# Attention and butterfly FFN on one core: the sums split into 64-key parts, one per row half of TensorE's array

## The reference, cut to what matters

```python
qkv = (x @ W_qkv + b_qkv).reshape(B, D, 3, H, p).transpose(2, 0, 3, 1, 4)
q, k, v = (qkv[0], qkv[1], qkv[2])
scores = jax.nn.softmax(jnp.einsum('bhip,bhjp->bhij', q, k), axis=-1)
out = jnp.einsum('bhij,bhjp->bhip', scores, v)
...
x = x + _L0_attn_ref(xn, ...) + _L0_ffn_ref(xn, ...)
```

## Time and profile before

| | us |
|---|---|
| median of 3 runs | 5605.22 |
| span of the profiled execution | 5607.5 |
| TensorE matmul busy | 5554.5 (99%) |
| ScalarE busy | 5021.6 (90%) |
| VectorE busy | 4884.1 (87%) |
| POOL busy | 527.8 (9%) |
| scores L1041, union busy, 8192 matmuls | 2058.5 |
| pieces L1019 without the difference, 7049 | 2497.4 |
| sums L1055, 16384 instructions | 2184.2 |
| exps L774, 8192 | 4222.8 |
| reductions L847, 6042 | 3958.3 |

### The profile page before, as it was taken

How to read it: one execution, slowest core, us unless ns; L and a number is a source line. 1 busy time by engine, 2 the same in 40 slices (tenths; PEclk the granted TensorE clock), 3 DMA queues, 4 the chain that set the end, 5 groups by cost and what they waited for, 6 DMA issues and landing times.

```text
span 5607.5 us, 98374 instructions
## 1 busy us (share of the span) xinstructions
PE 5554.5 (99%) x36132; PEld 2628.7 (47%) x36132; DVE 4884.1 (87%) x9092; ACT 5021.6 (90%) x9744; POOL 527.8 (9%) x482
## 2 busy tenths in 40 slices
PE   7899999999999999999999999999999999999999
PEld 6644444444444444444444444444444444444698
DVE  7799999999999999999999999999999999998233
ACT  6699999999999999999999999999999999999644
POOL 2436652000000000000000000000000000000000
PEclk9899999999999999999999999999999999999999
DMA  8702221111110111111111011111111101110111
GB/s 297 218 25 48 58 58 29 17 19 21 21 21 8 21 21 21 21 15 21 21 21 20 8 21 21 21 21 15 21 21 21 17 10 21 21 21 2 35 45 41
DMA packets 212351, 197.12 MB, mean 35 GB/s; under 512 B 149288, under 2 KB 170152, under 8 KB 200104
## 3 DMA queue, kind: packets, MB, share of 16 engines
q1 hardware_dynamic: 208432, 168.05, 15.9%
q0 software_dynamic: 3456, 23.07, 1.1%
HBM read 128.07 MB, written 60.82 MB: 34 GB/s over the span
## 4 chain that ended last, share of the span: by engine, by line
PE 96%; DVE 0%; issue 0%; DMA 0%; ACT 0%; SPq 0%; DVEq 0%; ACTq 0%
PE psum L1055 36%; PE psum L1019 32%; PE psum L1041 20%; PE psum L1142 3%; PE psum L1157 3%; PE psum L998 0%; DVE probs L856 0%; DMA q_rows<-neg_rows 0%; ACT probs L774 0%; PE psum L1073 0%; PE psum L1028 0%; PE psum L1080 0%; DVE maxima L856 0%; ACT L774 0%; DVE y L965 0%
## 5 line engine op out<-in xcount | busy, mean ns | idle before, releaser
L774 ACT ACTIVATE probs<-psum 128x512 f32<-128x512 f32 x8192 | 4222.8, 606 | 297.3 <-PE psum L1041 296.7
L847 DVE TENSOR_REDUCE maxima<-psum 128x1 f32<-128x512 f32 x6042 | 3958.3, 686 | 373.9 <-PE psum L1019 258.1
L1019 PE MATMUL psum<-k_rows,q_rows 48*128 48x512 f32 x7049 | 2497.4, 453 | 0.7 <-ACT spill L790 0.6
L1055 PE MATMUL psum<-probs,v_cols 128*32 128x512 f32 x16384 | 2184.2, 605 | 0.0
L1041 PE MATMUL psum<-q_rows,k_rows 50*128 50x512 f32 x8192 | 2058.5, 423 | 3.5 <-DMA q_rows<-neg_rows 3.5
L1019 PEld LDWEIGHTS psum<-k_rows,q_rows 48*128 48x128 f32 x7049 | 1175.4, 184 | 1244.0 <-DVE maxima L843 815.3
L1041 PEld LDWEIGHTS psum<-q_rows,k_rows 50*128 50x128 f32 x8192 | 1268.8, 185 | 126.0 <-ACT probs L774 33.2
L843 DVE CUSTOM_DVE_ANT_0 merged<-psum,spill 128x512 bf16<-128x512 f32 x1007 | 686.9, 682 | 1.8 <-issue 1.0
L790 ACT ACTIVATE spill<-psum 128x512 f32<-128x512 f32 x1007 | 602.0, 598 | 16.0 <-PE psum L1019 13.9
L1055 PEld LDWEIGHTS psum<-probs,v_cols 128*32 128x32 f32 x16384 | 322.5, 108 | 617.9 <-issue 323.7
L1019 PEld LDWEIGHTS psum<-k_diff,q_rows 48*128 48x128 f32 x1007 | 184.5, 183 | 845.7 <-DVE maxima L847 790.8
(11 more groups left out here) (106 smaller groups left out, 2154.0 us busy)
## 6 DMA issues: line engine op xcount, KB each, us to landing
q_rows<-q_parts SPq DMA_DIRECT2D x384, 128.0 KB, 4.4
k_rows<-k_parts SPq DMA_DIRECT2D x192, 128.0 KB, 7.1
q_parts<-parts SPq DMA_DIRECT2D x32, 512.0 KB, 6.4
k_parts<-parts SPq DMA_DIRECT2D x32, 512.0 KB, 4.1
planes<-in_up_planes POOLq DMA_DIRECT2D x10, 1024.0 KB, 6.7
planes<-in_down_planes POOLq DMA_DIRECT2D x10, 1024.0 KB, 5.0
y<-in_x SPq DMA_DIRECT2D x16, 512.0 KB, 5.1
xn_transposed<-xnt SPq DMA_DIRECT2D x16, 512.0 KB, 5.9
```

The source lines that it names most:

```text
L774: nc.scalar.activation(probs[:, 2 * (u % 2) + half, BANK * g:BANK * g + BANK], ps_s[:, r % 4, :], ACT.Exp).then_inc(s_exp, 1)
L847: nc.vector.tensor_reduce(largest, region(use), axis=AX_X, op=ALU.max).then_inc(s_region_free, 1)
L1019: nc.tensor.matmul(region(use_of[n, j]), q_rows[m % 4][lower:lower + ROWS, P * t:P * t + P], keys[lower:lower + ROWS, :], start=True, stop ...
L1055: last = nc.tensor.matmul(ps_o[VW * g:VW * g + VW, :], v_cols[:, KT * (head % 2) + UNITS * half + at, :], probs[:, 2 * (u % 2) + half, BAN ...
```

## The change

The 128 keys of a key half are split into 64 in partitions 0 to 63 and 64 in partitions 64 to 127. `sums(u, half, n)` multiplies one of these parts, with 64 rows by 32 columns, into its own bank: `ps_o[0]` (bank 6) for the lower rows, `ps_o[1]` (bank 7) for the upper. Scores keep 3 banks in place of 4, pieces keep 3 (now banks 3 to 5). There are twice as many calls of sums, with a counter for each row half.

The order of a unit becomes four equal quarters: the sums of one row part, and then two pieces and two scores that all lie in the other row half. `SCORE` and `PIECE` are permuted for it.

VectorE transposes both banks, into `o_t[0]` and `o_t[1]`; POOL adds the two (`join_and_scale`) before the reciprocal, which VectorE takes one unit later than before. To make room in SBUF for the second `o_t`, `fold` has two parts in place of three, and folding a butterfly stage takes 7 operations per row in place of 6 (a copy is added).

```diff
-    WEIGHT_OPS = 36
+    FOLD_OPS = 7
+    WEIGHT_OPS = 6 * FOLD_OPS
...
-        ps_s = psum[:, 0:4, :]
-        ps_max = psum[:, 4:7, :]
-        ps_o = psum[:, 7, :]
-        PIECE = [(1, 0), (1, 1), (0, 0), (1, 2), (0, 1), (0, 2), (1, 3), (0, 3)]
-        DIFFERENCE, MERGED = 3, 6
-        SCORE = [(r // 2 % 2, 2 * (r // 4) + r % 2) for r in range(2 * QG)]
+        SCORE_BANKS, REGION_BANKS = 3, 3
+        ps_s = psum[:, 0:SCORE_BANKS, :]
+        ps_o = [psum[:, SCORE_BANKS + REGION_BANKS + n, :] for n in range(2)]
+        PIECE = [(1, 0), (1, 1), (0, 0), (0, 1), (1, 2), (1, 3), (0, 2), (0, 3)]
+        DIFFERENCE, MERGED = 4, 5
+        SCORE = [(1 - r // 2 % 2, 2 * (r // 4) + r % 2) for r in range(2 * QG)]
...
-                def scale_and_add(s):
+                def join_and_scale(s):
+                    whole = o_t[0][:, :, 0:HD + 1]
+                    pool.wait_ge(s_o_free, 2 * s + 2)
+                    nc.gpsimd.tensor_tensor(whole, whole, o_t[1][:, :, 0:HD + 1], ALU.add).then_inc(s_o_whole, 1)
+                    pool.wait_ge(s_o_whole, s + 1)
                     pool.wait_ge(s_recip, s + 1)
...
                         if s > 0:
-                            sp.wait_ge(s_pv, KT * s)
+                            for n in range(2):
+                                sp.wait_ge(s_pv[n], KT * s)
...
                     if g == 0 and u >= 2:
-                        act.wait_ge(s_pv, 2 * (u - 2) + half + 1)
+                        for n in range(2):
+                            act.wait_ge(s_pv[n], 2 * (u - 2) + 2 - half)
...
                 def turn(s):
-                    dve.wait_ge(s_pv, KT * s + KT)
                     if s > 0:
                         dve.wait_ge(s_evac, s)
-                    nc.vector.transpose(o_t[:, :, :].rearrange("p t v -> p (t v)"), ps_o).then_inc(s_o_free, 1)
+                    for n in range(2):
+                        dve.wait_ge(s_pv[n], KT * s + KT)
+                        nc.vector.transpose(o_t[n][:, :, :].rearrange("p t v -> p (t v)"), ps_o[n]).then_inc(s_o_free, 1)
                 def invert(s):
-                    dve.wait_ge(s_o_free, s + 1)
-                    nc.vector.reciprocal(recip[:, :], o_t[:, :, HD]).then_inc(s_recip, 1)
+                    dve.wait_ge(s_o_whole, s + 1)
+                    nc.vector.reciprocal(recip[:, :], o_t[0][:, :, HD]).then_inc(s_recip, 1)
...
-                        if s > 0 and u == 0 and j == 1:
+                        if s > 0 and u == 1 and j == 1:
                             invert(s - 1)
...
-                    if e >= 4:
-                        pe.wait_ge(s_exp, e - 3)
+                    if e >= SCORE_BANKS:
+                        pe.wait_ge(s_exp, e - SCORE_BANKS + 1)
...
-                def sums(u, half):
+                def sums(u, half, n):
                     s, at = divmod(u, UNITS)
                     head = s // 2
-                    if at == 0 and half == 0:
+                    rows = slice(HALF_P * n, HALF_P * n + HALF_P)
+                    if at == 0 and half == 1:
                         if s > 0:
-                            pe.wait_ge(s_o_free, s)
+                            pe.wait_ge(s_o_free, 2 * (s - 1) + n + 1)
...
                     for g in range(QG):
-                        last = nc.tensor.matmul(ps_o[VW * g:VW * g + VW, :], v_cols[:, KT * (head % 2) + UNITS * half + at, :],
-                                                probs[:, 2 * (u % 2) + half, BANK * g:BANK * g + BANK],
-                                                start=(at == 0 and half == 0), stop=(at == UNITS - 1 and half == 1))
-                    last.then_inc(s_pv, 1)
+                        last = nc.tensor.matmul(ps_o[n][VW * g:VW * g + VW, :], v_cols[rows, KT * (head % 2) + UNITS * half + at, :],
+                                                probs[rows, 2 * (u % 2) + half, BANK * g:BANK * g + BANK],
+                                                start=(at == 0 and half == 1), stop=(at == UNITS - 1 and half == 0))
+                    last.then_inc(s_pv[n], 1)
...
-                    piece(n, 0)
-                    score(u + 1, 0)
-                    piece(n, 1)
-                    score(u + 1, 1)
-                    score(u + 1, 2)
-                    piece(n, 2)
-                    score(u + 1, 3)
-                    sums(u, 0)
-                    piece(n, 3)
-                    piece(n, 4)
-                    score(u + 1, 4)
-                    score(u + 1, 5)
-                    piece(n, 5)
-                    score(u + 1, 6)
-                    score(u + 1, 7)
-                    piece(n, 6)
-                    piece(n, 7)
-                    sums(u, 1)
+                    for quarter in range(4):
+                        sums(u, 1 - quarter // 2, quarter % 2)
+                        piece(n, 2 * quarter)
+                        score(u + 1, 2 * quarter)
+                        piece(n, 2 * quarter + 1)
+                        score(u + 1, 2 * quarter + 1)
```

More of the change, by code:

```diff
@@ L478, in attention_and_butterfly_ffn @@
         k_diff += [sb("k_diff1", [P, BANK], F32R, until=before_ffn)]
-        o_t = sb("o_t", [P, QT, VW], until=before_ffn)
+        o_t = [sb(f"o_t{n}", [P, QT, VW], until=before_ffn) for n in range(2)]
         neg_max = sb("neg_max", [P, QT], until=before_ffn)
@@ L485, in attention_and_butterfly_ffn @@
         planes = sb("planes", [P, 2, 4, PAIRS], until=before_ffn)
-        fold = sb("fold", [P, 3, PAIRS], until=before_ffn)
+        fold = sb("fold", [P, 2, PAIRS], until=before_ffn)
         merged = sb("merged", [P, BANK], BF16, until=before_ffn)
@@ L559, in attention_and_butterfly_ffn @@
         s_exp = sem("exps_done")
-        s_pv = sem("probs_used")
+        s_pv = [sem(f"probs_used_in_rows_of_half{n}") for n in range(2)]
         s_o_free = sem("sums_transposed")
+        s_o_whole = sem("sums_of_both_row_halves")
         s_recip = sem("sums_inverted")
@@ L655, in tmp @@
                         return fold[:, q, :].rearrange("p (n s) -> p n s", s=stride)
-                    if k % 6 == 0:
+                    step = k % FOLD_OPS
+                    if step == 0:
                         if r == 0:
@@ L687, in _ @@
                 for s in range(SUPER):
-                    for k in range(WEIGHT_OPS * s, min(WEIGHT_OPS * s + WEIGHT_OPS, 6 * len(rows_of_turns))):
+                    for k in range(WEIGHT_OPS * s, min(WEIGHT_OPS * s + WEIGHT_OPS, FOLD_OPS * len(rows_of_turns))):
                         fold_weights(k)
-                    scale_and_add(s)
+                    join_and_scale(s)
                 pool.wait_ge(s_evac, SUPER)
@@ L923, in _ @@
                 dve.wait_ge(s_lowest, 1)
-                for n in range(TILES_ALL + AHEAD + 1):
+                for n in range(TILES_ALL + AHEAD + 2):
                     m, t = divmod(n, QT)
@@ L1149, in down @@
                     else:
-                        pe.wait_ge(s_o_free, SUPER)
+                        pe.wait_ge(s_o_free, 2 * SUPER)
                         pe.wait_ge(s_bias, 1)
```

39 lines of the change are left out of this document (21 added, 18 removed).

## The result

The changed kernel takes 16440.14 us (median; 16438.99 to 16445.22) against 5605.43 us before in the same comparison: ratio 2.933, 95% interval 2.929 to 2.937. The prediction of 5490 us was wrong in sign, and the time lies outside its range and beyond every rival. The profiled execution has a span of 16437.4 us.

The account below looks back on a forecast made before the run. It took a ring of waits through TensorE, ScalarE and VectorE as the bound. 5607.5 - 171 (units) + 57 (super-step ends) - 4 (after the loop and last units) = 5489.5, predicted as 5490 us; case range 5300 to 5590, wider range 5300 to 7050.

Parts of the forecast that it names:

- the first end: TensorE's quarter: sums run fully beside the other half's pieces and scores, giving a 4.48 us unit.
- the other place: Bias matmuls before scores near 5226.2 us: two shapes, no overlap; read as array emptied or score 0 blocking issue.
- The overtaken piece 5: Second group of a unit before: scores 6 and 7 passed blocked piece 5, taken as evidence that halves queue separately.
- the second end: TensorE's quarter: sums do not overlap the other half's work at all, unit 8.44 us; chance 0.2.
- the 4.69 predicted: Unit time in us taken between 4.48 and 4.73, against 4.86 before; -171 us over 1007 units.
- the emptied array: Rival at each shape change: whole array drains, unit 8.44 us, 9250 us in all; chance 0.20.
- The ring: Unit's loop of waits through TensorE, ScalarE and VectorE, with three score banks: closes at 4.73 us.
- three banks take the gain: Rival at the score banks: overlap works, but bank turnaround makes the unit 4.89 us, 5690 us in all; chance 0.16.
- Ordered starts: Rival within a quarter: pieces start 0.45 us behind sums, unit 6.28 us, 7040 us; chance 0.10 including other half-overlaps.
- Super-step end: First sums of each super-step wait 1.26 us for the transpose in place of 0.36; +57 us over 63.
- POOL and SP: Super-step work: POOL's 64 adds (near 0.62 us), later reciprocal and SP's loads of V cost nothing in the loop.
- The length of a call: Sums: columns, not rows, set the time; 64-row calls keep 0.99 us, so sums grow from 2.0 to 4.0 us per unit.

Follow-up runs that it names:

- m1: TensorE alone, computing none of the reference: ten stages of 24 repeats without waits, begun from data at rest; run once, timed per stage.
- B: Stage on TensorE alone: fp32r 64x128 matmuls in both row halves in turn; 0.913 us per repeat of 8 matmuls.
- D: Stage on TensorE alone: calls of four 32-bit 64x32 matmuls in both row halves in turn; 0.859 us per two calls.
- G: Stage on TensorE alone: a 64x32 sums call beside four bf16 matmuls cut into 64x32, so one shape; 0.901 us per repeat.
- I: Stage on TensorE alone: a 32-bit 64x128 matmul beside four fp32r 64x128, one shape, two types; 0.892 us per repeat.
- E: Stage on TensorE alone: the changed kernel's quarter, halves swapped each time; 2.11 us at full clock, 3.86 us at half.
- m3: TensorE alone, ten stages of 24 repeats without waits, each started at half clock after 72 fp32r 64x128 matmuls in one half; no total time given.
- J: Stage on TensorE alone: as G with the bf16 matmuls uncut, so two shapes; 1.959 us per repeat at full clock.
- E8: Kernel before with three score banks in place of four and nothing else; 6804 us, ratio 1.215.
- e1: Changed kernel with the two 64-row parts of a sums call one after the other, half as many shape changes; 8971 us, 1.60 times before.
- e5: Kernel before with only the changed kernel's order of pieces and scores (128-row sums, four score banks kept); 6533 us, ratio 1.168.
- L: Stage on TensorE alone: one 64x32 call, then two fp32r 64x128 in each half; 1.653 us per quarter from full clock, 3.01 from half.
- C: Stage on TensorE alone: a call of four 32-bit 64x32 matmuls in the lower half only; 0.859 us per repeat.
- H: Stage on TensorE alone: the kernel before's pattern, 128x32 sums and then 64x128 in both halves; 2.12 us per half unit in m3.
- M: Stage on TensorE alone: 64x32 calls in both halves, then four fp32r 64x128 in one half and four in the other; 2.15 us per half unit.
- N: Stage on TensorE alone: as M with one 128x32 call for the sums; 2.13 us per half unit.
- O: Stage on TensorE alone: 64x32 calls in both halves, then eight fp32r 64x128 in turns; 2.15 us per half unit.
- Q: Stage on TensorE alone: 64x32 sums calls in one half only; no time given.
- S: Stage on TensorE alone: bf16 64x128 matmuls in one half only; no time given.
- T: Stage on TensorE alone: J run longer, the changed kernel's quarter with bf16; 1.959 us per quarter.
- A: Stage on TensorE alone: four fp32r 64x128 matmuls in the lower half; 1.54 us per repeat, mean over both clock levels.
- F: Stage on TensorE alone: as E with the halves never swapped; 2.11 us at full clock, 3.64 us mean over both levels.
- K: Stage on TensorE alone: four fp32r 64x128 in one half, halves swapped each time; 0.455 us per four matmuls.

## Why the prediction was wrong, point by point

**The failed step.** It is this one: "I take the first end, because overtaking between the halves is seen in every unit and the other place has a reading that leaves it whole". Sums of 64x32 do not run beside matmuls of 64x128 in the other row half. The overtaken piece 5 in the earlier trace rows was a true observation, but within one shape; m1's stages B, D, G and I confirm it. The bias matmuls in the earlier trace rows were the one place with two shapes and a row half free, and of its two readings "a change of shape empties the array" is the one that m1 shows for 64x32 and 64x128. For the bias matmuls' own shape, one row by 128 columns, no run tells the two readings apart. An event of the kind in question should have outweighed thousands of another kind. Of the two changes that follow, the first was priced in advance: the second end, 8.44 us per unit, is to the hundredth m1's 4 x 2.11. So 3.75 of the 10.75 us between the 4.69 predicted and the 15.44 measured belong to the lost overlap.

**What no case priced.** The other 7.00 us are the clock. The prediction carried's durations, all taken at the full clock, into a pattern that does not hold that clock; 9250 us for the emptied array and 1024 x 7.00 us are 16418, against 16440 measured. The sums go from 0.99 to 1.86 us, the group of four from 1.12 to 2.00. That E by itself falls from the full level (m1) and does not regain it (m3) is shown. Why it does, and why J with bf16 holds it, is not.

**The ring.** The 4.73 us were never tested in the changed kernel, where the other engines wait for TensorE. E8 shows that a ring on three banks is far dearer than I or the rival "three banks take the gain" (4.89 us) made it, in the order of before: 6.02 us. Both followed only the hand-over from piece to exp; the error was to leave out what is queued behind the waiting score. In the changed order a unit of e1 takes 6.13 us at the full clock with fully overlapping parts. So an array that did not empty would not have shown 5490 us for certain either; how much of those 6.13 is the banks and how much the order (5.77 us with four banks and 128-row sums, e5) was not taken apart.

**Ordered starts.** Refuted for these two shapes: the pieces come 1.86 us behind the sums (0.99 at the full clock), not 0.45. Within one shape matmuls do pass each other; the 16 instructions of sums in 1.03 us are in line with it.

**Super-step end.** Predicted 1.26 us per wait; measured 106.1 / 63 = 1.68 us, at half clock. The step had the right place and is 106 us against 79, small beside the rest. **POOL and SP.** As predicted they hold up nothing: POOL idles 14124 us before its adds, and these take 0.78 us where 0.62 was assumed.

**The length of a call.** Right: 64 rows stream as long as 128 (0.99 us per call in m1's E at the full clock), so splitting by rows doubles TensorE's work unless both halves run.

## What to carry to other kernels

Row halves of the array work beside each other only as long as both have tiles of one shape: before moving work into "the other half", look for one place in the trace with both shapes, and believe it over any number of places with one. Put what needs the full clock into a price only after the new pattern has been run by itself, from both levels. And count the PSUM banks given up for it: a score that waits for a bank holds up the sums queued behind it on TensorE, here 1.2 ms for one bank of four.

## What the runs showed of the hardware that was not expected

- TensorE, occupied for 15,774 us of 15,838, stayed at 1.2 GHz for all of that time. In e5, 98% occupied, it was at 2.4 GHz for all but 74 us.
- The level depends on where it was: L held 2.4 GHz for 118.7 us when it began there and stayed at 1.2 GHz for 72.3 us when it began there; C and J too kept whichever level they began at. Of the stages begun at the lower level, those that rose had both row halves, or whole rows, at work beside each other (B, D, H, M, N, O, within 5.2 us); those with one half alone did not (C, E, J), nor did L, whose sums stand alone in one half.
- One half alone does not always fall: C, J, Q, S and T held the full clock, A, E and F lost it 5, 9 and 6 us after their beginning, and so did A's kind of matmuls all ten times in m3. E differs from J, and A from S, only in the type of the 64x128 matmuls: fp32r in the stages that fell, bf16 in those that held. K has fp32r as A has, but both of its halves at work, and held.
- A 32-bit call of 64x32 in both halves (16 instructions) takes 0.859 us back to back, as long as one in a single half (0.859).
- What stays open: what makes the clock of e1 and e4 change level 99 and 153 times, when their patterns without waits (M, O) rise and hold. Their TensorE waits for exps and reductions, and no run took only these waits away.
